# Spectral stage of a MetaFormer block: the mixed spectrum is turned in blocks on VectorE instead of passing through DRAM, and the mixing is interleaved with the next unit's x products

## The chip, the cores and the metric

One NeuronCore of one Trainium2 chip. The metric is the device time of one launch in microseconds; the kernel before is given by the median of three runs.

## What is computed

The input x is (32 images, 64 channels, 56x56), float32. The reference, cut to what matters:

```python
x = x + conv_ref(ln_c(x), ...)          # binary 3x3 convolution, batch norm, residual
t = tokens(x)                           # (32, 3136, 64)
t = t + ffn_ref(ln_t(t), ...)
# ffn_ref, for each of 4 branches i (the first T, T/2, T/4, T/8 tokens):
#   U_plus  = irfft(rfft(phi, 4096) * rfft(u, 4096))[:, :sl]        for 16 filters
#   U_minus = the same with u * (-1)^t, times (-1)^t afterwards
#   out_i   = sum_k s_k U_plus_k @ M_plus[i, k] + s_k U_minus_k @ M_minus[i, k]
#             + sum_{j<3} shift(u, j) @ M_u[i, j]
# and the output is a sum over branches with one-hot weights
```

The kernel does the length-4096 transforms in two steps, 128 rows (64 slots) by 32. In between, at each frequency, the spectrum of x (32 images by 64 channels) is multiplied by a 64x64 complex matrix that is itself put together from 35 filters.

## The kernel before, in words

The program has four parts, one after the other: `prepare` (constants, filters), `norm_and_convolve` (both norms, the convolution, the first transform step; it leaves the result in DRAM as z), `mix_frequencies` (the part that the change touches) and `finish` (the last transform step, the sum with the residual, the output).

`mix_frequencies` (L905 to L1247) first folds the four branches' matrices into m_sta (L1118 to L1128 on TensorE, L1204 on ScalarE, L1242 on VectorE). Then it goes through 32 units. A unit is two slots, 64 complex frequencies (NF = 64). Its work is cut into chunks of one PSUM bank (512 float32 columns), in the order that PLAN (L871) gives:

- p_v (L1058): the filters' spectrum for the unit; VectorE scales it in two instructions (L1150, L1153) to v_mov.
- x, 4 chunks (L1066): the second forward step of x, 4 matmuls of 128 columns each, array used as 128x128. Four copies a chunk (L1168) take the bank apart into xf.
- h, 16 chunks (L1071): the filter products, 8 float16 matmuls of 128 columns each, on two column tiles (L1078). One copy a chunk (L1172) into hf, 128x512.
- inv, 4 chunks, of the unit two before (LAG_INV = 2): the first inverse step, 16 matmuls of 512 columns on tiles of 32 rows and 64 columns (L1105). Copied to wf (L1178).
- mix, 4 chunks (L1082): at each frequency xf times hf, 16 matmuls of 128 columns a chunk on four tiles of 32 columns (L1090). Copied to y_sb (L1175).

In the trace each float32 matmul appears as two MATMUL instructions, so a mix chunk is 32 of them, an x chunk 8, the inverse step 32.

The seven banks of `ring` are used in turn: chunk p writes bank p % 7 and waits until the chunk seven before it has been copied (`bank_free`, L1033). Chunks with even p are copied by ScalarE, odd p by VectorE (`saver`, L1139). Each engine does its chunks in the order of the plan; TensorE issues its own strictly in that order too, so a matmul that waits holds back all that come behind it.

The mixed spectrum needs its frequencies on the partitions for the inverse step. Before, this goes through DRAM: y_sb is stored to y_scratch (L964), and read back in another order into yt (L969), two buffers of each. These are 1 MB out and 1 MB in for each unit, on SyncE's queue, which also loads the next z (L957), the constants fwd and inv (L958, L961) and, once, after the first two units, four tiles of the residual (L990, `load_x1`). GpSimd stores wf to w_scratch in 8 DMAs a unit (L1020), waits for their landing and then raises w_free (L1024), for which the next copy into the one wf waits (L1161).

For the last units the head of a unit (p_v, x, h, mix) is over before the tail (inv), so two steps with nothing but an inverse step come at the end.

Of the kernel before, what the change touches and what calls it, by code (L numbers as in the profile page):

```python
# [88 lines left out]
def constants():  # L89
# [44 lines left out]
    inv = inv.transpose(0, 1, 4, 2, 3, 5).reshape(NUNIT, 2 * NALPHA, 128)  # L134
    inv = np.concatenate([inv, inv], 1)
# [735 lines left out]
PLAN = [("x", 4), ("h", 16), ("inv", 4), ("mix", 4)]  # L871
TAIL = ("inv",)
LAG_INV = 2
RING = 7


def unit_chunks():

    seen, out = {}, []
    for stage, count in PLAN:  # L880
        for _ in range(count):
            k = seen.get(stage, 0)
            seen[stage] = k + 1
            out.append((stage, k, len(out)))
    return out


def chunk_is_there(stage, u):

    return (u >= LAG_INV) if stage in TAIL else (u < NUNIT)  # L890


def chunks_until(u, p, engine=None):


    plan = unit_chunks()
    if isinstance(u, int):
        return sum(1 for w in range(u + 1) for stage, _, at in plan
                   if chunk_is_there(stage, w) and (w < u or at <= p) and engine in (None, at % 2))
    per_unit = sum(1 for _, _, at in plan if engine in (None, at % 2))  # L900
    missing = LAG_INV * sum(1 for stage, _, at in plan if stage in TAIL and engine in (None, at % 2))
    return per_unit * u - missing + sum(1 for _, _, at in plan if at <= p and engine in (None, at % 2))


def mix_frequencies(nc, d, keep):  # L905


    chunks = unit_chunks()
    NCH = len(chunks)
    assert NCH % RING == 0 and NCH % 2 == 0  # L910
    pos = {(s, k): p for s, k, p in chunks}
    with ExitStack() as own:
# [8 lines left out]
        inv = [sb(f"inv{i}", [128, 2, 2 * NA]) for i in range(2)]  # L921
# [16 lines left out]
        y_stored = [sem(f"y_stored{i}") for i in range(2)]  # L938
        y_loaded = [sem(f"y_loaded{i}") for i in range(2)]
        chunk_ready, v_ready, v_saved, w_stored, w_free = (  # L940
            sem(n) for n in ("chunk_ready", "v_ready", "v_saved", "w_stored", "w_free"))
        sp_turn, pool_turn = sem("sp_turn"), sem("pool_turn")
# [12 lines left out]
        def _(sp):  # L955
# [4 lines left out]
            def load_inv(u, slot):  # L960
                sp.dma_start(inv[slot][:].rearrange("p r f -> p (r f)"), d["c_inv"][u]).then_inc(inv_loaded[slot], 16)  # L961

            def store_y(slot):
                sp.dma_start(d["y"][slot].rearrange("i p n -> p i n"), y_sb[slot][:]).then_inc(y_stored[slot], 16)  # L964

            def load_y(slot):
                for h in range(2):
                    src = d["y"][slot].rearrange("i (j m) n -> (i j) m n", j=4)[:, 16 * h:16 * h + 16, :]
                    sp.dma_start(yt[slot][64 * h:64 * h + 64].rearrange("p m r e -> p (m r e)"),  # L969
                                 src.rearrange("f m n -> f (m n)")).then_inc(y_loaded[slot], 16)  # L970
# [40 lines left out]
        def _(pool):  # L1011
            def store(u):

                for e in range(2):
                    pool.wait_ge(saved[e], chunks_until(u + LAG_INV, pos["inv", 3], e))
# [12 lines left out]
            with pool.Fori(1, NUNIT - LAG_INV) as u:  # L1028
                store(u)
            for u in range(NUNIT - LAG_INV, NUNIT):  # L1030
                store(u)

        def bank_free(eng, u, p):  # L1033

            if not isinstance(u, int):
                w, at = (u, p - RING) if p >= RING else (u - 1, p - RING + NCH)
                eng.wait_ge(saved[at % 2], chunks_until(w, at, at % 2))
                return
            before = [(w, at) for w in range(u + 1) for stage, _, at in chunks
                      if chunk_is_there(stage, w) and at % RING == p % RING and (w < u or at < p)]  # L1040
            if before:
                w, at = before[-1]
                eng.wait_ge(saved[at % 2], chunks_until(w, at, at % 2))
# [7 lines left out]
        def _(pe):  # L1051
            def unit(u, slot, use, head, tail):
# [7 lines left out]
                for stage, k, p in chunks:  # L1060
                    if not (tail if stage in TAIL else head):
                        continue
                    if stage != "inv":
                        bank_free(pe, u, p)
                    bank = ring[:, p % RING, :]
                    if stage == "x":  # L1066
                        for j in range(4):
                            at = CH * (8 * k + 2 * j)
                            mm = nc.tensor.matmul(bank[:, 128 * j:128 * j + 128], z_in[slot][:, at:at + 2 * CH],  # L1069
                                                  fwd[slot][:, NF:3 * NF], start=True, stop=True)  # L1070
                    elif stage == "h":  # L1071
# [3 lines left out]
                        for i in range(4):  # L1075
                            e = 4 * k + i
                            for n in range(2):
# [3 lines left out]
                                    tile_position=(0, CH * n))  # L1081
                    elif stage == "mix":  # L1082
                        if k == 0:
                            all_saved(pe, u, pos["h", 15])
                            if is_first(u):
                                pe.wait_ge(reals_done, 3)
                        for i in range(4):
                            for j in range(4):
                                f = 16 * k + 4 * i + j
                                mm = nc.tensor.matmul(bank[32 * j:32 * j + 32, 128 * i:128 * i + 128], xf[:, f, :],  # L1090
                                                      hf[:, f, :, :].rearrange("p r e -> p (r e)"),
                                                      start=True, stop=True, tile_position=(0, 32 * j))
                    else:
# [5 lines left out]
                        pe.wait_ge(y_loaded[slot], 32 * (use - 1))  # L1099
                        pe.wait_ge(inv_loaded[slot], 16 * (use - 1))  # L1100
                        for c in range(2):
                            for r in range(2):
                                for n in range(4):
                                    rows = slice(32 * n, 32 * n + 32)
                                    mm = nc.tensor.matmul(  # L1105
                                        ring[64 * c:64 * c + 64, pos["inv", n] % RING, :], inv[slot][rows, r, :],
                                        yt[slot][rows, 8 * c:8 * c + 8, r, :], start=(r == 0), stop=(r == 1),
                                        tile_position=(32 * n, 64 * c))
                                    if c and r:
# [364 lines left out]
```

## Time and profile before

| | us |
|---|---|
| median of 3 runs | 1436.41 |
| lowest, highest | 1433.49, 1443.66 |
| the profiled execution: time | 1433.59 |
| its span, first to last instruction | 1431.9 |
| mean granted TensorE clock in it | 0.931 of 2.4 GHz |

The profile was taken of one execution. Its busy figures are shares of the whole span, and mix the four parts, which have different limits; the unit loop lies at about 629 to 1182 us of the span. PE is TensorE's matmuls, DVE VectorE, ACT ScalarE, POOL GpSimd, SP SyncE. "idle before <- releaser" says how long an engine stood still ahead of an instruction and what ended that.

### The profile page before, as it was taken

To read this page: it belongs to the slowest core of one execution; us is meant where nothing else is said; L and a number is where in the kernel's file an instruction comes from. 1 tells how busy PE (TensorE), PEld (TensorE's weight loads), DVE (VectorE), ACT (ScalarE), POOL (GpSimd) and SP (SyncE) were. 2 spreads that over 40 slices of the span, in tenths; PEclk is the share of its full clock that TensorE was granted. 3 is DMA by queue.
4 is the path that set the end of the run, shared out by engine and by line. 5 is a ranking of instruction groups with operands and counts; after the bars stand their busy time and mean duration, and the time that the engine had idled before them with its cause. 6 is when DMAs were issued, how large, how long until landed. Compare 5 with 4: busy or idle time off the path is not lost. (4 is left out here: it accounts for less than half of the span.)

```text
span 1431.9 us, 37537 instructions
## 1 busy us (share of the span) xinstructions
PE 1174.5 (82%) x15089; PEld 779.4 (54%) x15089; DVE 954.0 (67%) x1420; ACT 798.9 (56%) x1487; POOL 498.9 (35%) x440
## 2 busy tenths in 40 slices
PE   1899999999999977688698998999899926865667
PEld 1455555555555543147577777777777713433334
DVE  5288888888888888636477777677777713433334
ACT  1787788778887853335366666566656612322223
POOL 2146556666655567200122332232232230000000
PEclk9999999999999988669899999999999977988778
DMA  7024545554455448426899999899989969978873
GB/s 228 1 91 133 166 155 182 188 162 149 154 181 172 149 133 185 140 82 187 263 281 300 270 283 299 272 275 291 291 267 284 284 177 359 406 313 341 327 314 135
DMA packets 179624, 317.66 MB, mean 222 GB/s; under 512 B 14805, under 2 KB 154423, under 8 KB 162935
## 3 DMA queue, kind: packets, MB, share of 16 engines
q1 hardware_dynamic: 164966, 257.47, 56.6%
q0 software_dynamic: 14592, 59.26, 11.8%
q8 instruction: 47, 0.77, 0.2%
q14 instruction: 19, 0.16, 0.0%
HBM read 162.93 MB, written 153.76 MB: 221 GB/s over the span
## 5 line engine op out<-in xcount | busy, mean ns | idle before, releaser
L1020 POOL DMA_DIRECT2D w_scratch<-wf x256 | 151.2, 594 | 430.5 <-ACT y_sb L1197 391.5
L491 POOL TENSOR_TENSOR u_t<-u_t,root 98x1024 f32<-98x1024 f32 x62 | 118.0, 1935 | 169.2 <-DVE root L799 169.2
L535 PE MATMUL ring_norm<-x_all,center 128*128 128x448 f32 (+2 forms) x384 | 148.1, 511 | 24.9 <-PEq L211 15.7
L1402 ACT ACTIVATE out_sb<-p_turn 128x392 f32<-128x392 f32 x128 | 62.7, 498 | 189.6 <-PE p_turn L1358 177.7
L1346 PE MATMUL p_out<-w_in,last_masked 128*98 128x512 f32 x256 | 141.2, 636 | 23.8 <-DMA w_in<-w_scratch 23.8
L1078 PE MATMUL ring<-v_mov,m_sta 105*64 105x128 f16 x4096 | 147.2, 221 | 14.3 <-DVE xf L1213 11.6
L1213 DVE COPY hf<-ring 128x512 f32<-128x512 f32 x256 | 156.1, 682 | 1.0
L1197 ACT ACTIVATE hf<-ring 128x512 f32<-128x512 f32 x256 | 144.7, 597 | 4.9
L1391 DVE TENSOR_TENSOR x_in<-p_out,x_in 98x512 f32<-98x512 f32 x96 | 65.4, 690 | 123.1 <-DMA x_in<-x_scratch 68.3
L594 PE MATMUL ring_norm<-u_t,step_masked 98*128 98x512 f32 x256 | 126.7, 623 | 21.9 <-POOL u_t L491 21.9
L1078 PEld LDWEIGHTS ring<-v_mov,m_sta 105*64 105x64 f16 x4096 | 119.9, 110 | 40.2 <-DVE xf L1213 16.8
L1090 PE MATMUL ring<-hf,xf 128*32 128x128 f32 x4096 | 123.3, 278 | 19.1 <-ACT wf L1197 8.8
L1090 PEld LDWEIGHTS ring<-hf,xf 128*32 128x32 f32 x4096 | 113.0, 112 | 45.0 <-issue 30.6
L491 POOL TENSOR_TENSOR xc_t<-xc_t,root 98x1024 f32<-98x1024 f32 x64 | 119.7, 1900 | 50.7 <-DVE root L799 50.7
L1197 ACT ACTIVATE xf<-ring 64x256 f32<-64x256 f32 x256 | 98.5, 385 | 66.8 <-PE ring L1069 64.5
L1213 DVE COPY xf<-ring 64x256 f32<-64x256 f32 x256 | 108.2, 423 | 32.4 <-PE ring L1069 28.1
L1069 PE MATMUL ring<-fwd,z_in 128*128 128x128 f32 x1024 | 122.2, 279 | 0.0
L1069 PEld LDWEIGHTS ring<-fwd,z_in 128*128 128x128 f32 x1024 | 121.7, 196 | 0.1
L535 PEld LDWEIGHTS ring_norm<-x_all,center 128*128 128x128 f32 x384 | 66.6, 192 | 84.5 <-issue 44.9
L1358 PEld LDWEIGHTS p_turn<-ident,x_in 98*128 98x128 f32 x384 | 47.1, 153 | 120.1 <-DVE x_in L1391 67.5
L567 PE MATMUL p_conv<-signs_padded,conv_w 64*64 64x392 bf16 x2304 | 109.2, 330 | 0.2 <-DVE x_all L755 0.2
L624 ACT ACTIVATE xc_t<-ring_norm 98x512 f32<-98x512 f32 x128 | 78.7, 615 | 46.1 <-PE ring_norm L546 46.1
(132 smaller groups left out, 1923.1 us busy)
## 6 DMA issues: line engine op xcount, KB each, us to landing
z_in<-z_scratch SPq DMA_DIRECT2D x32, 1076.5 KB, 9.7
z_scratch<-z_sb SPq DMA_DIRECT2D x16, 2048.0 KB, 8.9
y_scratch<-y_sb SPq DMA_DIRECT2D x32, 1024.0 KB, 12.7
yt<-y_scratch SPq DMA_DIRECT2D x64, 512.0 KB, 6.2
w_scratch<-wf POOLq DMA_DIRECT2D x256, 128.0 KB, 7.6
w_in<-w_scratch SPq DMA_DIRECT2D x8, 4096.0 KB, 15.8
x_all<-in_x SPq DMA_DIRECT2D x16, 1568.0 KB, 7.6
x_scratch<-x_t SPq DMA_DIRECT2D x16, 1568.0 KB
```

The lines of the kernel that those rows point to most:

```text
L491: return eng.tensor_tensor(v, v, r, ALU.mult)
L535: nc.tensor.matmul(bank_of("cen", q, c)[:, 0:WID * n], keep["center"][:, h, :], x_of(q)[:, WID * row:WID * row + WID * n], start=True, sto ...
L567: mm = nc.tensor.matmul(bank[CH * out:CH * out + CH, h, 0:CW], keep["conv_w"][CH * k:CH * k + CH, t, CH * k:CH * k + CH], pad[q % 2][CH * ...
L594: nc.tensor.matmul(bank_of("z", q, c), keep["step1"][:, c // 2, :], u_t[q % 2][:, c, :], start=True, stop=True).then_inc(z_ready, 1)
L624: nc.scalar.activation(xc_t[q % 2][:, c, :], bank, ACT.Copy).then_inc(xt_copied, 1)
L1020: nc.gpsimd.dma_start(w_units[u, h, s, c], wf[64 * c:64 * c + 64, 2 * h + s].rearrange("p (g n) -> p g n", n=256)).then_inc(w_stored, 16)
L1069: mm = nc.tensor.matmul(bank[:, 128 * j:128 * j + 128], z_in[slot][:, at:at + 2 * CH], fwd[slot][:, NF:3 * NF], start=True, stop=True)
L1078: mm = nc.tensor.matmul(bank[CH * n:CH * n + CH, 2 * NF * i:2 * NF * i + 2 * NF], m_sta[:, e, :], v_mov[:, NF * (1 - n):NF * (3 - n)], sta ...
L1090: mm = nc.tensor.matmul(bank[32 * j:32 * j + 32, 128 * i:128 * i + 128], xf[:, f, :], hf[:, f, :, :].rearrange("p r e -> p (r e)"), start= ...
L1197: return nc.scalar.activation(dst, src, ACT.Copy)
L1213: return nc.vector.tensor_copy(dst, src)
L1346: nc.tensor.matmul(p_out[0:NB, c % BANKS, :], keep["last"][:, ACH * c // MASKG, :], w_in[w_slot][:, ACH * c:ACH * c + ACH, 128 * slot:128 ...
```

## The change

The order of a step u becomes: p_v(u); then mix chunk k of unit u-1 and x chunk k of unit u in turn, for k = 0 to 3; then (on VectorE) four turns of the mixed spectrum of u-1; then the 16 h chunks of u; then the inverse step of u-1. The lag is one unit (LAG = 1), and one step with the tail alone is left at the end.

The four mix chunks stay in four PSUM banks (3 to 6), and VectorE turns them from there in 32x32 blocks into yt, a quarter of the channels in each of four `transpose` instructions of 512 elements in each partition. y_sb, y_scratch and their DMAs are gone. The inverse step is 8 matmuls of 512 columns on tiles of 64 rows and 64 columns, its constants are one tile of 64 columns. xf gets a second buffer, yt has one.

Banks and copying engines are given by tables; in `bank_free` a bank that held a mix chunk counts as free once the last turn is done. ScalarE copies x 0 and 2, eleven h chunks and inv 0 and 2; VectorE copies x 1 and 3, h 2, 5, 8, 11 and 14 and inv 1 and 3, and does the turns.

```diff
-PLAN = [("x", 4), ("h", 16), ("inv", 4), ("mix", 4)]
-TAIL = ("inv",)
-LAG_INV = 2
+TAIL = ("mix", "turn", "inv")
+LAG = 1
 RING = 7
+FIRST_MIX = 3
+H_ON_VECTOR = (2, 5, 8, 11, 14)
+BANKS = {"mix": (3, 4, 5, 6), "x": (0, 1, 2, 0), "h": (1, 2, 0, 1, 2, 0, 3, 4, 5, 6, 1, 2, 0, 3, 4, 5),
+         "inv": (6, 1, 2, 0)}
+def owner(stage, k):
+    if stage == "turn":
+        return 1
+    return int(k in H_ON_VECTOR) if stage == "h" else k % 2
+def step_chunks():
+    out = []
+    for k in range(4):
+        out += [("mix", k), ("x", k)]
+    out += [("turn", k) for k in range(4)]
+    out += [("h", k) for k in range(16)]
+    out += [("inv", k) for k in range(4)]
+    return [(stage, k, p) for p, (stage, k) in enumerate(out)]
...
-        xf = sb("xf", [128, NF, NIMG])
+        xf = [sb(f"xf{i}", [128, NF, NIMG]) for i in range(2)]
-        y_sb = [sb(f"y_sb{i}", [128, NF // 4, 2 * CH]) for i in range(2)]
-        yt = [sb(f"yt{i}", [128, NIMG // 2, 2, CH]) for i in range(2)]
+        yt = sb("yt", [128, CH, NIMG])
...
             def body(u, slot, use):
+                sp.wait_ge(chunk_ready, chunks_until(u, pos["x", 3]))
+                after_wait(sp, sp_turn)
                 if not known(u, NUNIT - 2, NUNIT - 1):
-                    sp.wait_ge(chunk_ready, chunks_until(u, pos["x", 3]))
-                    after_wait(sp, sp_turn)
                     load(u + 2, slot)
-                for e in range(2):
-                    sp.wait_ge(saved[e], chunks_until(u, pos["mix", 3], e))
-                after_wait(sp, sp_turn)
-                store_y(slot)
                 if not known(u, 0, 1):
                     load_inv(u, slot)
-                sp.wait_ge(y_stored[slot], 16 * use)
-                after_wait(sp, sp_turn)
-                load_y(slot)
...
+            stage, k, _ = chunks[at]
+            if stage == "mix":
+                stage, k, at = chunks[pos["turn", 3]]
+            eng.wait_ge(saved[owner(stage, k)], chunks_until(w, at, owner(stage, k)))
...
-                            all_saved(pe, u, pos["h", 15])
+                            all_saved(pe, u - 1, pos["h", 15])
-                                f = 16 * k + 4 * i + j
-                                mm = nc.tensor.matmul(bank[32 * j:32 * j + 32, 128 * i:128 * i + 128], xf[:, f, :],
+                                f = 16 * j + 4 * k + i
+                                mm = nc.tensor.matmul(bank[32 * j:32 * j + 32, 128 * i:128 * i + 128],
+                                                      xf[1 - slot][:, f, :],
+                                                      hf[:, f, :, :].rearrange("p r e -> p (r e)"),
...
-                        pe.wait_ge(y_loaded[slot], 32 * (use - 1))
-                        pe.wait_ge(inv_loaded[slot], 16 * (use - 1))
-                        for c in range(2):
-                            for r in range(2):
-                                for n in range(4):
-                                    rows = slice(32 * n, 32 * n + 32)
-                                    mm = nc.tensor.matmul(
-                                        ring[64 * c:64 * c + 64, pos["inv", n] % RING, :], inv[slot][rows, r, :],
-                                        yt[slot][rows, 8 * c:8 * c + 8, r, :], start=(r == 0), stop=(r == 1),
-                                        tile_position=(32 * n, 64 * c))
+                        pe.wait_ge(saved[1], chunks_until(u, pos["turn", 3], 1))
+                        pe.wait_ge(inv_loaded[1 - slot], 16 * (use if slot else use - 1))
+                        after_wait(pe, pe_turn)
+                        for h in range(2):
+                            for c, row in ((0, 0), (1, 1), (1, 0), (0, 1)):
+                                images = slice(16 * h + 8 * c, 16 * h + 8 * c + 8)
+                                rows = slice(64 * row, 64 * row + 64)
+                                mm = nc.tensor.matmul(
+                                    bank_of("inv", 2 * h + row)[64 * c:64 * c + 64, :],
+                                    inv[1 - slot][rows, :], yt[rows, :, images],
+                                    start=True, stop=True, tile_position=(64 * row, 64 * c))
...
-                    if p % 2 != which or not (tail if stage in TAIL else head):
+                    if (stage, k) not in mine or not (tail if stage in TAIL else head):
                         continue
-                    eng.wait_ge(chunk_ready, chunks_until(u, p))
+                    eng.wait_ge(chunk_ready, chunks_until(u, pos["mix", 3] if stage == "turn" else p))
                     if (stage, k) == ("inv", first_inv):
-                        eng.wait_ge(w_free, u - 1)
+                        eng.wait_ge(w_free, u)
...
-                        copy(y_sb[slot][:, 4 * k:4 * k + 4, :].rearrange("p i n -> p (i n)"), bank
+                    elif stage == "turn":
+                        e = slice(16 * k, 16 * k + 16)
+                        nc.vector.transpose(
+                            yt[:, e, :], ring[:, FIRST_MIX:FIRST_MIX + 4, :]
+                            .rearrange("p b (i r e) -> p e r (b i)", r=2, e=CH)[:, e]).then_inc(saved[which], 1)
+                    else:
+                        copy(wf[:, k, :].rearrange("p (i e) -> p i e", e=CH), bank.rearrange("p (e i) -> p i e", e=CH)
                              ).then_inc(saved[which], 1)
```

## Rows read from the trace of the kernel before

**Rows 1.** The page: busy time of TensorE; granted clock and DMA share in 40 slices

```profile
PE 1174.5 (82%) x15089; PEld 779.4 (54%) x15089; DVE 954.0 (67%) x1420; ACT 798.9 (56%) x1487; POOL 498.9 (35%) x440
...
PEclk9999999999999988669899999999999977988778
DMA  7024545554455448426899999899989969978873
```

**Rows 2.** Busy time of each engine, clock, DMA share, GB/s: 100 us of units

```profile
900.00:1000.00 100.00, 90.99 (x2021) 76.28 (x2021) 74.55 (x144) 62.99 (x131) 31.14 (x53) 1.00 0.91 281
```

**Rows 3.** Timeline of one unit: start us, us, engine line op, what, count [idle before]

```profile
868.37 0.57 PE L1058 MATMUL p_v<-fwd,z_in 128*105 128x192 f32 x2
...
868.78 3.73 PE L1069 MATMUL ring<-fwd,z_in 128*128 128x128 f32 x32
...
869.87 1.57 ACT L1197 ACTIVATE xf<-ring 64x256 f32<-64x256 f32 x4 [1.64 <-PE ring L1069]
...
870.76 3.52 DVE L1213 COPY xf<-ring 64x256 f32<-64x256 f32 x8 [0.79 <-PE ring L1069]
...
872.44 1.53 PE L1078 MATMUL ring<-v_mov,m_sta 105*64 105x128 f16 x48
873.26 4.65 ACT L1197 ACTIVATE hf<-ring 128x512 f32<-128x512 f32 x8
874.31 4.88 DVE L1213 COPY hf<-ring 128x512 f32<-128x512 f32 x8
...
878.42 2.01 PE L1105 MATMUL ring<-yt,inv 32*64 32x512 f32 x32 [0.93 <-DVE hf L1213]
...
880.36 3.70 PE L1090 MATMUL ring<-hf,xf 128*32 128x128 f32 x128
...
880.64 1.29 DVE L1213 COPY wf<-ring 128x512 f32<-128x512 f32 x2 [1.45 <-PE ring L1105]
...
883.99 0.57 PE L1058 MATMUL p_v<-fwd,z_in 128*105 128x192 f32 x2
```

**Rows 4.** Timeline, TensorE, same unit: last start of x, inverse step, mix

```profile
872.24 0.28 PE L1069 MATMUL ring<-fwd,z_in 128*128 128x128 f32 x1
...
879.75 0.67 PE L1105 MATMUL ring<-yt,inv 32*64 32x512 f32 x8
...
883.76 0.29 PE L1090 MATMUL ring<-hf,xf 128*32 128x128 f32 x4
```

**Rows 5.** The page, costliest groups: the convolution on tiles of 64x64

```profile
L567 PE MATMUL p_conv<-signs_padded,conv_w 64*64 64x392 bf16 x2304 | 109.2, 330 | 0.2 <-DVE x_all L755 0.2
```

**Rows 6.** Timeline, TensorE, the first five units

```profile
628.69 0.97 PE L1058 MATMUL p_v<-fwd,z_in 128*105 128x192 f32 x2 [1.56 <-DVE m_sta L1242]
...
643.06 3.70 PE L1090 MATMUL ring<-hf,xf 128*32 128x128 f32 x128 [2.51 <-DVE hf L1187]
646.69 0.57 PE L1058 MATMUL p_v<-fwd,z_in 128*105 128x192 f32 x2
...
682.49 2.36 PE L1090 MATMUL ring<-hf,xf 128*32 128x128 f32 x39 [4.85 <-issue]
...
709.57 1.94 PE L1090 MATMUL ring<-hf,xf 128*32 128x128 f32 x32 [8.27 <-ACT wf L1197]
...
728.14 0.57 PE L1058 MATMUL p_v<-fwd,z_in 128*105 128x192 f32 x2
```

**Rows 7.** Timeline, the end of the stage: last copies and store of wf, first load of `finish`

```profile
1170.69 1.29 DVE L1213 COPY wf<-ring 128x512 f32<-128x512 f32 x2 [8.58 <-PE ring L1105]
...
1172.56 4.68 POOL L1020 DMA_DIRECT2D w_scratch<-wf  x8 [5.17 <-DVE wf L1213]
1182.29 0.81 SPq L1284 DMA_DIRECT2D w_in<-w_scratch  x2
```

**Rows 8.** Clock after a wait: the timeline's matmuls, then engines and clock of 1 us

```profile
657.66 5.37 PE L1090 MATMUL ring<-hf,xf 128*32 128x128 f32 x128 [1.85 <-DVE hf L1213]
...
659.00:660.00 1.00, 1.00 (x25) 1.00 (x21) 0.00 (x0) 0.60 (x1) 0.00 (x0) 0.50 0.92 258
```

More of the change, by code:

```diff
@@ L888, in chunk_is_there @@
 def chunk_is_there(stage, u):
-    return (u >= LAG_INV) if stage in TAIL else (u < NUNIT)
+    return (u >= LAG) if stage in TAIL else (u < NUNIT)
 def chunks_until(u, p, engine=None):
-    plan = unit_chunks()
+    if engine is None:
+        mine = [(stage, at) for stage, k, at in step_chunks() if stage != "turn"]
+    else:
+        mine = [(stage, at) for stage, k, at in step_chunks() if stage != "mix" and owner(stage, k) == engine]
     if isinstance(u, int):
-        return sum(1 for w in range(u + 1) for stage, _, at in plan
-                   if chunk_is_there(stage, w) and (w < u or at <= p) and engine in (None, at % 2))
@@ L900, in chunks_until @@
-    per_unit = sum(1 for _, _, at in plan if engine in (None, at % 2))
-    missing = LAG_INV * sum(1 for stage, _, at in plan if stage in TAIL and engine in (None, at % 2))
-    return per_unit * u - missing + sum(1 for _, _, at in plan if at <= p and engine in (None, at % 2))
+        return sum(1 for w in range(u + 1) for stage, at in mine
+                   if chunk_is_there(stage, w) and (w < u or at <= p))
+    missing = LAG * sum(1 for stage, at in mine if stage in TAIL)
+    return len(mine) * u - missing + sum(1 for stage, at in mine if at <= p)
@@ L905, in mix_frequencies @@
 def mix_frequencies(nc, d, keep):
-    chunks = unit_chunks()
-    NCH = len(chunks)
-    assert NCH % RING == 0 and NCH % 2 == 0
+    chunks = step_chunks()
     pos = {(s, k): p for s, k, p in chunks}
@@ L1027, in _, with bank_of @@
             store(0)
-            with pool.Fori(1, NUNIT - LAG_INV) as u:
+            with pool.Fori(1, NUNIT - LAG) as u:
                 store(u)
-            for u in range(NUNIT - LAG_INV, NUNIT):
+            for u in range(NUNIT - LAG, NUNIT):
                 store(u)
+        def bank_of(stage, k):
+            return ring[:, BANKS[stage][k], :]
         def bank_free(eng, u, p):
+            stage, k, _ = chunks[p]
+            same = [at for other, n, at in chunks if other != "turn" and BANKS[other][n] == BANKS[stage][k]]
             if not isinstance(u, int):
[L1036 to L1041, printed above, removed]
+                w, at = (u, max(at for at in same if at < p)) if min(same) < p else (u - 1, max(same))
+            else:
+                before = [(w, at) for w in range(u + 1) for at in same
+                          if chunk_is_there(chunks[at][0], w) and (w < u or at < p)]
+                if not before:
+                    return
                 w, at = before[-1]
-                eng.wait_ge(saved[at % 2], chunks_until(w, at, at % 2))
+            stage, k, _ = chunks[at]
+            if stage == "mix":
+                stage, k, at = chunks[pos["turn", 3]]
+            eng.wait_ge(saved[owner(stage, k)], chunks_until(w, at, owner(stage, k)))
         def all_saved(eng, u, p):
@@ L1060, in unit @@
                 for stage, k, p in chunks:
-                    if not (tail if stage in TAIL else head):
+                    if stage == "turn" or not (tail if stage in TAIL else head):
                         continue
@@ L1064, in unit @@
                         bank_free(pe, u, p)
-                    bank = ring[:, p % RING, :]
+                    bank = bank_of(stage, k) if stage != "inv" else None
                     if stage == "x":
@@ L1130, in _ @@
             two_by_two(pe, NUNIT, body)
[L1131 to L1132 removed]
+            unit(NUNIT, NUNIT % 2, NUNIT // 2 + 1, False, True)
         def m_part(c):
@@ L1139, in saver @@
         def saver(eng, which, copy):
-            mine = [(stage, k) for stage, k, p in chunks if p % 2 == which]
+            mine = [(stage, k) for stage, k, p in chunks if stage != "mix" and owner(stage, k) == which]
             first_inv = min(k for stage, k in mine if stage == "inv")
-            first_mix = min(k for stage, k in mine if stage == "mix")
             last_h = max(k for stage, k in mine if stage == "h")
@@ L1205, in _ @@
             unit = saver(act, 0, copy)
-            two_by_two(act, NUNIT, lambda u, slot, use: unit(u, slot, use, True, not known(u, 0, 1)))
-            for u in (NUNIT, NUNIT + 1):
-                unit(u, u % 2, u // 2 + 1, False, True)
+            two_by_two(act, NUNIT, lambda u, slot, use: unit(u, slot, use, True, not known(u, 0)))
+            unit(NUNIT, NUNIT % 2, NUNIT // 2 + 1, False, True)
         @block.vector
@@ L1244, in _ @@
             unit = saver(dve, 1, copy)
-            two_by_two(dve, NUNIT, lambda u, slot, use: unit(u, slot, use, True, not known(u, 0, 1)))
-            for u in (NUNIT, NUNIT + 1):
-                unit(u, u % 2, u // 2 + 1, False, True)
+            two_by_two(dve, NUNIT, lambda u, slot, use: unit(u, slot, use, True, not known(u, 0)))
+            unit(NUNIT, NUNIT % 2, NUNIT // 2 + 1, False, True)
 def finish(nc, d, keep):
```

57 lines of the change are left out of this document (17 added, 40 removed).

## The prediction

> **What bounds the kernel now.** I read the page's slices first: the clock and the DMA share [rows 1] show a stage with the clock at full and the DMA engines nine tenths busy, the unit loop. Then the engines over 100 us of it [rows 2]: TensorE 91%, VectorE 75%, ScalarE 63%, DMA share 0.91. The DMA is loaded but ends nothing in the steady part; what does, the timeline of one unit says [rows 3]. From one p_v to the next it is 883.99 - 868.37 = 15.62 us, all of it TensorE's chain: p_v 0.41, x 3.66, h with its waits 5.98 (872.44 to 878.42), inverse step 1.94, mix 3.63. The waits inside are short, 0.93 us at most. So in the steady part the trip of y through DRAM costs nothing: it lies beside a chain of matmuls.
>
> It costs at the ends. In the first five units [rows 6] there are idle times of 4.85 and 8.27 us; from 646.69 to 728.14 there are four units, 81.45 us where four times 15.62 is 62.5: 19.0 us are lost, while the residual's four tiles and y share the DMA engines. At the end two steps with a tail alone wait for y. The whole stage, first p_v to the first load of `finish`, is 1182.29 - 628.69 = 553.6 us [rows 6, 7].
>
> **The change, a step at a time.** Time 0 is the start of p_v, warm clock.
>
> TensorE's slots. The 32 x instructions start from 868.78 to 872.24 [rows 3, 4], a pitch of 0.1116, so a chunk of 8 is 0.89. Mix: 124 instructions from 880.36 to 883.76, 0.0274 each, 0.88 a chunk of 32 (0.89 taken). h is 48 in 1.53 less the last one's length, 0.028 each: 0.225 a chunk of 8. The inverse step keeps its number of rounds: 8 tiles of 32x64 with 32 instructions, now 4 tiles of 64x64 with 16; four rounds of 0.43 either way, 1.75. That four 64x64 tiles do run at once the convolution bears out: 109.2 us / 2304 = 47 ns for 392 columns [rows 5].
>
> Change of tile shape. Over and above the pitch, the first matmul of the next kind comes late by 872.44 - 872.24 - 0.11 = 0.09 (x to h), 883.99 - 883.76 - 0.11 = 0.12 (mix to p_v), 880.36 - 879.75 - 0.43 = 0.18 (inverse to mix) [rows 3, 4]. I take 0.10. There are four such changes in a unit now, eleven in the new step. The Trainium skill (TensorEngine Tiling (Array Packing), Key Properties) says that changing the tiling mode drains TensorE; this speaks against alternating mix and x, and by the rows the seven added drains are 0.7 us a step, at 0.18 each 1.3. The trace agrees that there is a price, and puts it at these tenths.
>
> First part, to the end of the last x chunk: 0.1 + 0.37 + 4 x 0.89 + 4 x 0.89 + 8 x 0.10 = 8.4 us. The two waits in it are covered: banks 0 to 2 are free of the inverse chunks by then, x 3 needs x 0's bank, copied at 4.2.
>
> Then comes what I think decides. VectorE has its work in this order: v_mov, x 1, x 3, the four turns, and only then h 2. The pieces in line:
> - x 3 is ready at 8.6 (0.2 after its last slot, as 869.87 is after the first chunk's [rows 3]); four copies at 3.52 / 8 = 0.44 each: 10.3.
> - Four turns, 512 elements each from PSUM. No row shows one. The nearest is VectorE's copy of 512 elements out of PSUM, eight in 4.88, 0.61 each [rows 3]; I take 0.62, to 12.8. Below, the 256-element copy at 0.44 (18.4 a step instead of 19.2); above, a turn that reads its block first and writes it after, twice the copy, 1.22 (21.6 a step). The Trainium skill (Vector Engine (DVE) Microarchitecture Reference, section 3.8) has the block transpose sustain one element per cycle per lane; as an estimate from that page a turn is some 0.53 us and the step 18.8. No run here shows it yet.
> - h 2's copy: 13.4. TensorE meanwhile issued h 0 and h 1 (to 8.9), stood until x 3's bank 0 came free (10.4), issued h 2 to h 4 (to 11.1), and stands again: h 5 needs bank 0, which h 2 holds, whose copy is behind the turns. It starts at 13.5. Everything behind h 5 waits with it, also h 6 to h 9, whose banks 3 to 6 the turns freed.
> - From there ScalarE sets the pace: h 6, 7, 9, 10 and 12 at 0.58 each (4.65 us for eight [rows 3]) from 13.9: h 12 is copied at 17.0. The inverse step needs the banks of h 9 to h 12, starts 0.4 later (now 0.4 lie between h 11's copy and it: 874.31 + 5 x 0.60 + 0.68 = 878.0 against 878.42 [rows 3]), and takes 1.75 to 19.2.
>
> So a step is 19.2 us against 15.62. VectorE is busy only some 12 us of it and ScalarE 11; it is their order, not their load, that makes 5.3 us of TensorE's idle time in a step.
>
> The edits that come out at nothing: y's store and load, hidden now, so nothing gained in a steady unit; load_inv and the next z are issued after x 3 with a whole step to land; the copies into wf have the same shape as before (0.60 a copy, strided reads are there in h's already); v_mov is done at 1.7 and needed at 8.5. SyncE loses a wait, which frees nobody. GpSimd's eight stores are ready a step before w_free is wanted.
>
> **Sum over the stage.** Step 0 has no tail: from p_v to the first mix after it 643.06 - 628.69 = 14.4 us before [rows 6], the same now within a few tenths (14.2: the next p_v goes ahead of that wait). 31 steps of P follow. Then the step with a tail alone: mix 3.9, turns 2.5, inverse step 2.3. Its copy into wf waits for the store before it (ready 1.8 after the step starts, 4.7 to issue [rows 7], some 5 to land: 11.8), copies end at 13.1, and from last copy to `finish` it is 10.3 (1182.29 less 1170.69 + 1.29 [rows 7]): 23.4. The stage is 37.6 + 31 P. The 19.0 us lost at the start aren't in it: with y's 2 MB a unit gone, I take the residual's tiles to find room. With P = 19.2 it is 632.8, 79 more than 553.6. It would break even at P = 16.6.
>
> The clock. It is at 2.4 GHz through the units, with a wait of 0.9 in each. After a wait of 1.85 us it went to 1.2 GHz once, and the mix took 5.37 instead of 3.70, 1.67 more [rows 8]; after one of 2.51 it stayed up [rows 6]. The new step has waits of 1.5 and 2.4 us with only 0.7 us of matmuls between them, and 1.4 more ahead of the inverse step. Bounds: nothing, or 1.67 in each step. The slow stretch would fall first on the h products, where ScalarE sets the pace and half speed costs little, so I take 0.7. P = 19.9, the stage 37.6 + 616.9 = 654.5, 100.9 more.
>
> The profiled execution took 1433.6 (2.8 below the median, 0.2%): 1433.6 + 100.9 = 1534.5, and I say 1535 us.
>
> **Rivals.**
> A. The same chain, clock at 2.4 GHz throughout: P = 19.2, 1433.6 + 79 = 1513 us. For it: the 2.51 us wait after which the clock held. Against: here two waits come together, in every step.
> B. The clock falls and stays low into the inverse step and the next mix: P = 20.9, the stage 685.5, 1565 us. For: the 1.67 measured.
> C. A turn costs twice a copy: P = 21.6 + 0.3 of clock, the stage 716, 1596 us. For: nothing in the trace but that the operation is new; the copies' rate is the likelier guide.
> D. Faster. The turns are hidden, h isn't held, and TensorE runs on as now; 15.62 + 0.7 for shape changes = 16.3, the stage 543, 1423 us. The gain is then the DMA's at both ends. It needs 2.6 us off the chain from x 3's copy to h 12's copy, so turns and copies on VectorE that overlap far more than the 0.61 pitch shows. Against: VectorE's order is written down, and h 5's bank hangs on it.
> E. It doesn't do what it says, DMA load stays: the DMA's waits return at the start, 19 us on the forecast, 1554. Inside the range and hardly likely, as the stores are deleted.
>
> **Numbers.** Forecast 0.39, A 0.22, B 0.18, C 0.09, D 0.07, E 0.02; 0.03 for about no change, which lies between D and A. The range from 1488 (turns at 0.44 and a held clock: P = 18.4) to 1590 leaves out D, most of C and no change. A difference of 1% (14 us) is about what can be told from none: slower 0.90, same 0.03, faster 0.07.
>
> **What would show it.** Right: p_v to p_v near 20 us; TensorE waiting for VectorE's hf copy ahead of an h product for over 2 us in each step, and for its xf copy for 1.5; transposes near 0.68 each, four in 2.5; ScalarE's h copies in two bunches; DMA share about half; clock under 1.0 in a part of each step; no idle time of 4 us or more in the first units. Wrong: h products that run without those waits, transposes of 1.2, or a step under 17 us.

## The result, and the profile after

The changed kernel takes 1557.68 us, median of 4 runs (1557.04 to 1558.24), against 1434.95 for the one before in the same rounds: a ratio of 1.0843, 95% interval 1.0802 to 1.0885. It is slower, by 8%, where 1535 was forecast (range 1488 to 1590).

The page of the changed kernel, the lines that answer to [rows 1]:

```profile
PE 1253.8 (81%) x14577; PEld 824.8 (53%) x14577; DVE 944.0 (61%) x1388; ACT 812.8 (52%) x1519; POOL 499.2 (32%) x440
...
PEclk9999999999999875788888888888888886988878
DMA  7025546464555473263333334333333326988883
```

and 200 us of steps, to set beside [rows 2] (busy us of TensorE, its weight loads, VectorE, ScalarE, GpSimd; clock; DMA share; GB/s):

```profile
800.00:1000.00 200.00, 164.86 (x2964) 130.32 (x2956) 111.89 (x206) 100.20 (x205) 43.41 (x74) 0.85 0.36 109
```

The DMA share fell from 0.91 to 0.36: the change does what it says. VectorE has less to do per microsecond than before (56% against 75%), ScalarE too, and TensorE is idle or slow. The clock, 1.00 in the units before, is 0.85.

The timeline of one step says where the time went (start us, length us, engine, line, operation, count, idle before and its releaser); it answers to [rows 3]:

```profile
894.56 0.57 PE L1060 MATMUL p_v<-fwd,z_in 128*105 128x192 f32 x2
...
900.27 1.16 PE L1071 MATMUL ring<-fwd,z_in 128*128 128x128 f32 x8
...
901.36 1.08 PE L1094 MATMUL ring<-hf,xf 128*32 128x128 f32 x32
...
902.37 1.16 PE L1071 MATMUL ring<-fwd,z_in 128*128 128x128 f32 x8
...
903.46 0.64 PE L1081 MATMUL ring<-v_mov,m_sta 105*64 105x128 f16 x16
...
903.57 1.73 DVE L1215 COPY xf<-ring 64x256 f32<-64x256 f32 x4 [2.47 <-PE ring L1071]
...
905.33 2.51 DVE L1176 STREAM_TRANSPOSE yt<-ring 128x512 f32<-128x512 f32 x4
...
905.35 0.86 PE L1081 MATMUL ring<-v_mov,m_sta 105*64 105x128 f16 x24 [1.25 <-DVE xf L1215]
...
907.76 0.65 DVE L1215 COPY hf<-ring 128x512 f32<-128x512 f32 x1
...
908.47 4.90 PE L1081 MATMUL ring<-v_mov,m_sta 105*64 105x128 f16 x88 [2.26 <-DVE hf L1215]
...
913.30 2.15 PE L1111 MATMUL ring<-yt,inv 64*64 64x512 f32 x16
...
915.38 0.57 PE L1060 MATMUL p_v<-fwd,z_in 128*105 128x192 f32 x2
```

VectorE copies x 3 (1.73), turns (2.51), copies h 2 (0.65), in one row without a gap; TensorE waits first for the x 3 copy (1.25 us) and then for h 2's (2.26), and only at 908.47 goes on with h 5. Those are the two waits of the forecast. Steps come in a cycle of 19.96, 20.82 and 20.65; nine of them from 1078.87 to 1263.19 make 20.48 each, against 15.62 before.

The clock of single microseconds of that step: around the second wait, among the h products and in the next p_v:

```profile
906.00:907.00 1.00, 0.21 (x8) 0.05 (x2) 1.00 (x3) 0.97 (x2) 0.00 (x0) 0.96 1.00 422
907.00:908.00 1.00, 0.00 (x0) 0.00 (x0) 1.00 (x3) 0.11 (x1) 0.00 (x0) 0.50 0.96 398
...
912.00:913.00 1.00, 1.00 (x24) 1.00 (x22) 0.41 (x2) 0.87 (x2) 0.00 (x0) 0.50 0.00 0
915.00:916.00 1.00, 1.00 (x14) 0.38 (x10) 0.83 (x2) 0.74 (x2) 0.00 (x0) 1.00 0.00 0
```

It falls to 1.2 GHz just before 907, within the second wait, stays there past 913, through h 5 to h 15, and is back at 2.4 for the float32 products. The h products at half clock take 4.90 us for 11 chunks, 0.44 a chunk; so TensorE, not the copies, sets the pace there. The waits are the same in every step, and the low stretch is not: about 6.3 us here, 6.8 in the step of 20.65, and 3.9 in the one of 19.96, where the clock falls at about 889.9, behind the wait and in the middle of the h products:

```profile
888.51 3.71 PE L1081 MATMUL ring<-v_mov,m_sta 105*64 105x128 f16 x88 [2.26 <-DVE hf L1215]
...
892.15 2.48 PE L1111 MATMUL ring<-yt,inv 64*64 64x512 f32 x16
```

The ends of the stage, which answer to [rows 6, 7]: the first p_v, a wait for GpSimd's store of wf, the first load of `finish`.

```profile
628.37 0.97 PE L1060 MATMUL p_v<-fwd,z_in 128*105 128x192 f32 x2 [1.56 <-DVE m_sta L1244]
...
689.22 2.08 PE L1071 MATMUL ring<-fwd,z_in 128*128 128x128 f32 x8 [3.04 <-DVE wf L1215]
...
1303.99 0.80 SPq L1285 DMA_DIRECT2D w_in<-w_scratch  x2
```

The stage takes 1303.99 - 628.37 = 675.6 us, 122.0 more than before; the whole execution 1557.15, 123.6 more than the one before. All of the loss is in this stage.

### The profile page after: what moved, and what is told of

It reads as the page before. It is cut to its first block and busy times, and to the rows that moved or that the text cites. A ratio compares the mean times of both kernels' runs of the same rounds, so it can differ in the third digit from the quotient of the medians.

```text
span 1554.8 us, 36484 instructions
## 1 busy us (share of the span) xinstructions
PE 1253.8 (81%) x14577; PEld 824.8 (53%) x14577; DVE 944.0 (61%) x1388; ACT 812.8 (52%) x1519; POOL 499.2 (32%) x440
## 5 line engine op out<-in xcount | busy, mean ns | idle before, releaser
L1081 PE MATMUL ring<-v_mov,m_sta 105*64 105x128 f16 x4096 | 189.6, 271 | 110.3 <-DVE hf L1215 70.3
L1200 ACT ACTIVATE hf<-ring 128x512 f32<-128x512 f32 x352 | 190.1, 598 | 144.0 <-PE ring L1081 143.4
L1081 PEld LDWEIGHTS ring<-v_mov,m_sta 105*64 105x64 f16 x4096 | 171.6, 145 | 124.7 <-DVE hf L1215 75.5
L1071 PE MATMUL ring<-fwd,z_in 128*128 128x128 f32 x1024 | 152.4, 294 | 3.0 <-DVE wf L1215 3.0
L1215 DVE COPY hf<-ring 128x512 f32<-128x512 f32 x160 | 109.2, 684 | 65.9 <-PE ring L1081 65.7
L1071 PEld LDWEIGHTS ring<-fwd,z_in 128*128 128x128 f32 x1024 | 128.6, 197 | 27.9 <-issue 24.4
L1094 PE MATMUL ring<-hf,xf 128*32 128x128 f32 x4096 | 139.3, 278 | 1.8 <-DVE hf L1190 1.8
L1094 PEld LDWEIGHTS ring<-hf,xf 128*32 128x32 f32 x4096 | 105.4, 110 | 21.9 <-issue 8.0
```

What stands on the lines that cost most here:

```text
L1081: mm = nc.tensor.matmul(bank[CH * n:CH * n + CH, 2 * NF * i:2 * NF * i + 2 * NF], m_sta[:, e, :], v_mov[:, NF * (1 - n):NF * (3 - n)], sta ...
L1200: return nc.scalar.activation(dst, src, ACT.Copy)
L1215: return nc.vector.tensor_copy(dst, src)
```

## The experiments

Theory: the order of VectorE's queue (x 3, four turns, h 2) holds up h 5 and all behind it, and the waits let the clock fall. Rivals: the alternation of tile shapes, the amount of work on VectorE, the DMA.

**e1_h_owner: no h copy behind the turns**

```diff
-H_ON_VECTOR = (2, 5, 8, 11, 14)
+H_ON_VECTOR = (7, 9, 11, 13, 15)
```

> The changed kernel with one table altered: VectorE copies h chunks 7, 9, 11, 13 and 15 instead of 2, 5, 8, 11 and 14, so that no h chunk that comes before h 6 has its copy behind the four turns. If VectorE's queue order is the cause, the wait of 2.3 us ahead of h 5 goes, one of under 1 us is left ahead of h 6 (banks 3 to 6 come free with the last turn), and a step falls from 20.5 to about 18.4 us: 1557.7 - 31 x 2.1 = 1493 us. If the alternation of tile shapes or the mere amount of work on the copying engines is the cause (the amounts are the same), the time stays within 10 us of 1557.7.

Measured: 1544 us (1537 and 1551), ratio 1.0743 (1.0657 to 1.0829) to the kernel before. 14 us gained where 65 were expected, and the two runs lie 14 apart. The timeline has the reason. The waits did change as expected, 1.26 ahead of h 2, 0.24 ahead of h 5, 1.02 ahead of h 6 for the last turn. But the steps come in two kinds. From 706.10 to 874.96 they are 18.2 and 19.2 in turn, nine of them 18.76 on average; from 895 on they grow from 20.29 to 20.48 and stay there. Clock and busy times of a stretch of either kind, and of one step of 18.2:

```profile
820.00:857.00 37.00, 31.37 (x604) 24.59 (x608) 22.19 (x42) 20.36 (x42) 9.42 (x16) 0.95 0.41 123
...
762.75:780.97 18.22, 15.11 (x311) 11.67 (x307) 11.10 (x21) 9.97 (x21) 4.72 (x8) 1.00 0.41 125
...
1017.00:1058.00 41.00, 35.96 (x620) 27.52 (x612) 22.99 (x43) 20.84 (x43) 9.43 (x16) 0.83 0.37 111
```

The h products from h 6 on, in a step of 19.2, in one of 18.2 and in one of 20.29:

```profile
756.89 4.05 PE L1081 MATMUL ring<-v_mov,m_sta 105*64 105x128 f16 x80 [1.02 <-DVE yt L1176]
...
776.08 2.42 PE L1081 MATMUL ring<-v_mov,m_sta 105*64 105x128 f16 x80 [1.02 <-DVE yt L1176]
...
908.39 4.48 PE L1081 MATMUL ring<-v_mov,m_sta 105*64 105x128 f16 x80 [1.02 <-DVE yt L1176]
...
912.79 2.61 PE L1111 MATMUL ring<-yt,inv 64*64 64x512 f32 x16
```

The same program, with the same waits: in the steps of 18.2 the clock does not fall at all, in those of 19.2 it is low for some 3.4 us, in the later ones for some 6.8 us, all the h products from h 6 on and a part of the inverse step (2.61 against 1.95). The 18.4 that was expected is met by the steps at full clock. At 20.48 the later steps are no shorter than the changed kernel's: there the low clock costs 20.48 - 18.22 = 2.26 us and takes back the whole gain. What the order is worth can't be read from this run beside the changed kernel's, since both order and clock differ; e2_filled and e7_owner_filled hold the clock.

**e2_filled: the clock held**

```diff
+WARM = {2: 5, 5: 9}
...
+                    if stage == "h" and k in WARM:
+                        for _ in range(WARM[k]):
+                            nc.tensor.matmul(p_v[:, 256:384], keep["center"][:, 0, :], keep["center"][:, 0, :],
+                                             start=True, stop=True)
```

> The changed kernel with matmuls that nobody reads put into TensorE's two waits, five 128-column float32 ones ahead of h 2 and nine ahead of h 5, 1.1 and 2.0 us where it stood for 1.25 and 2.26. If the low clock on the h products is a cost of those waits, the granted clock stays at 1.00 through the step, h 5 to h 15 go at ScalarE's pace again, and a step falls by 0.9 to 1.3 us: 1557.7 - 31 x 1.1 = about 1524 us. If the clock costs nothing because the copies set the pace anyway, the time stays within 8 us of 1557.7.

Measured: 1523.9 us, ratio 1.0602 (1.0537 to 1.0667); 1524 was expected. Each step is 19.27 (999.82 to 1192.51 are ten). The end of one step, the h products after the filled wait in the next, and the clock:

```profile
898.78 3.54 ACT L1205 ACTIVATE hf<-ring 128x512 f32<-128x512 f32 x7 [2.03 <-PE ring L1086]
...
901.61 1.95 PE L1116 MATMUL ring<-yt,inv 64*64 64x512 f32 x16 [0.86 <-ACT hf L1205]
...
917.40 2.65 PE L1086 MATMUL ring<-v_mov,m_sta 105*64 105x128 f16 x88
```

```profile
917.00:920.00 3.00, 2.95 (x92) 2.64 (x90) 2.49 (x5) 1.92 (x4) 0.00 (x0) 1.00 0.14 40
```

88 instructions take 2.65 us, not 4.90, and now the copies set the pace: the inverse step waits 0.86 us for ScalarE. h 2 and h 5 start as far behind p_v as without the unneeded matmuls (10.79 and 13.91), so these held up nothing. Work that nobody needs made the kernel 34 us faster. So of the 4.86 us that a step has lost, 1.21 are the clock, and 3.65 are there at full clock.

**e7_owner_filled: both**

The edit is e1_h_owner's table in e2_filled, with `WARM = {2: 5, 6: 4}`.

> e1_h_owner and e2_filled together: no h copy behind the turns ahead of h 7, and five and four matmuls that nobody reads ahead of h 2 and of h 6, to hold the clock. e1_h_owner alone shortened TensorE's waits by 1 us a step and gained nearly nothing, its steps 20.48 us with the h products at the low clock. If that was the clock, here it is 1.00 and the step some 17.6 us against e2_filled's 19.27: 1523.9 - 31 x 1.65 = 1473 us. If the order of the copies was never worth anything, it stays at 1524 within 10.

Measured: 1492.1 us, ratio 1.0395 (1.0373 to 1.0418). A step is 18.24 (1002.23 to 1148.12 are eight), 1.03 below e2_filled's; 1.65 was expected. The direction is right and the size is not. With the clock held the copies' order is worth a microsecond a step, and 31 x 1.03 = 32 us is what was measured. The steps of e1_h_owner in which the clock did not fall, 18.22, say the same. It does not clear the path, since h 6 still waits for the turns, which hold banks 3 to 6:

```profile
905.09 1.16 PE L1068 MATMUL p_v<-center 128*128 128x128 f32 x8
...
906.18 2.42 PE L1086 MATMUL ring<-v_mov,m_sta 105*64 105x128 f16 x80
```

**e3_turns_twice: the turns doubled**

```diff
-                        nc.vector.transpose(
-                            yt[:, e, :], ring[:, FIRST_MIX:FIRST_MIX + 4, :]
-                            .rearrange("p b (i r e) -> p e r (b i)", r=2, e=CH)[:, e]).then_inc(saved[which], 1)
+                        for dst in (spare, yt):
+                            ins = nc.vector.transpose(
+                                dst[:, e, :], ring[:, FIRST_MIX:FIRST_MIX + 4, :]
+                                .rearrange("p b (i r e) -> p e r (b i)", r=2, e=CH)[:, e])
+                        ins.then_inc(saved[which], 1)
```

> The changed kernel with each of the four turns made twice, the first time into a tile that nobody reads: 2.5 us more on VectorE in each step. If the turns lie in the one chain that sets the step, the step grows by 1.7 to 2.5 us and the time by 53 to 80 us, to 1611 to 1638. If they lie beside something longer, the time stays within 15 us of 1557.7.

Measured: 1646.8 us, ratio 1.1458 (1.1385 to 1.153), 89 above the changed kernel, 9 over the upper end. The clock's mean fell from 0.887 to 0.866 in it. TensorE's wait ahead of h 5 is 4.65 us instead of 2.26, so the 2.5 us of four turns are on the path nearly in full, and the clock, lower in the mean, goes with the rest: 89 / 32 = 2.8 us a step.

**e5_not_alternating: shapes in blocks, clock held**

```diff
-    for k in range(4):
-        out += [("mix", k), ("x", k)]
+    out += [("mix", k) for k in range(4)]
+    out += [("x", k) for k in range(4)]
     out += [("turn", k) for k in range(4)]
```

This on top of e2_filled.

> e2_filled (clock held by matmuls that nobody reads) with the four mix chunks first and the four x chunks after them; the turns stay behind x 3 on VectorE, all tables as they are. This takes six of the changes of tile shape out of a step and moves nothing else in the chain. From e2_filled's trace p_v to h 0 is 8.90 us; with blocks as e4_turn_under_x has them (0.50 + 3.63 + 3.92) it is 8.05. Expected: a step of 18.4 us where e2_filled has 19.27, and 1523.9 - 31 x 0.85 = 1497 us. If the shape changes are hidden behind the copies, 1524 within 6.

Measured: 1506.7 us (1500 and 1513), ratio 1.0496 (1.0438 to 1.0554). A step is 18.75 (1006.25 to 1137.50 are seven), 0.52 under e2_filled's; 0.85 was expected. One step of the trace shows where the rest went:

```profile
893.75 0.57 PE L1061 MATMUL p_v<-fwd,z_in 128*105 128x192 f32 x2
...
903.66 2.51 DVE L1181 STREAM_TRANSPOSE yt<-ring 128x512 f32<-128x512 f32 x4
...
904.95 2.27 PE L1068 MATMUL p_v<-center 128*128 128x128 f32 x18
906.10 0.65 DVE L1220 COPY hf<-ring 128x512 f32<-128x512 f32 x1
...
907.15 2.65 PE L1086 MATMUL ring<-v_mov,m_sta 105*64 105x128 f16 x88
```

The turns start 9.91 us after p_v, where the changed kernel has 10.77: 0.86 earlier, as expected, 0.14 for each of the six changes. But h 5 starts only 0.51 earlier. The copy that frees its bank ends at 906.75, and the nine unneeded matmuls, written for the longer wait, run on to 907.2. So the step understates what the changes of shape cost. The two runs lie 13 us apart, and nothing on record says why; the step is read from the faster one. The changes of shape count, and they are the smaller part of the 3.65 us.

**e6_y_sixteenth: the kernel before, nearly without y**

```diff
-                store_y(slot)
+                part = 16 if known(u, 0, 1) else 1
+                store_y(slot, part)
...
-                load_y(slot)
+                load_y(slot, part)
```

From the third unit on the inverse step reads old values in most of yt.

> The kernel before, with y stored and loaded in full for the first two units only and a sixteenth of it from the third on, so the inverse step of later units reads old values in most of yt: 1.9 MB less DMA in each unit. If y's trip is hidden in the steady part, as the prediction has it, a unit stays at 15.6 us and only the start (19.0 us lost) and the end gain, together 10 to 30 us: 1437 goes to 1407 to 1427. If the DMA load slows the units themselves, a unit falls below 15.4 and the time below 1400.

Measured: 1429.9 us, ratio 0.994 (0.9916 to 0.9963). A unit is 15.59 (1011.61 to 1136.30 are eight), as before. The trip through DRAM costs nothing in the steady part; that half of the expectation held. The other did not, and 1430 lies above the 1407 to 1427 that was expected: the start is as bad as it was, although y is gone from the third unit on:

```profile
682.48 1.85 PE L1092 MATMUL ring<-hf,xf 128*32 128x128 f32 x39 [4.03 <-issue]
...
711.94 1.94 PE L1092 MATMUL ring<-hf,xf 128*32 128x128 f32 x32 [9.69 <-ACT wf L1199]
```

**e4_turn_under_x: the turns beside the x products**

```diff
-    for k in range(4):
-        out += [("mix", k), ("x", k)]
+    out += [("mix", k) for k in range(4)]
     out += [("turn", k) for k in range(4)]
+    out += [("x", k) for k in range(4)]
...
-H_ON_VECTOR = (2, 5, 8, 11, 14)
+H_ON_VECTOR = (3, 5, 7, 9, 11)
...
-"x": (0, 1, 2, 0), "h": (1, 2, 0, 1, 2, 0, 3, 4, 5, 6, 1, 2, 0, 3, 4, 5),
-         "inv": (6, 1, 2, 0)}
+"x": (2, 0, 1, 2), "h": (3, 4, 5, 6, 0, 1, 2, 3, 4, 5, 6, 0, 1, 2, 3, 4),
+         "inv": (5, 6, 0, 1)}
```

> All four mix chunks first, then the four x chunks: VectorE turns the mixed spectrum while TensorE makes x, and TensorE finds banks 3 to 6 free when h begins. h chunks go through the seven banks in turn, VectorE copies h 3, 5, 7, 9 and 11. If the place of the turns in VectorE's queue is the cause, TensorE's waits of over 1 us are gone, the clock stays at 1.00, and a step is about 15.5 us: 1557.7 - 31 x 5.0 = 1403 us, faster than both kernels. If only the changes of tile shape count, six fewer at under 0.2 us each, it is 1557.7 - 31 x 1.1 = 1524 us.

Measured: 1414.2 us, ratio 0.9839 (0.9787 to 0.9891): 9% under the changed kernel and 1.6% under the one before. The step is 15.59, the clock 1.00 in it. The turns run while TensorE makes x:

```profile
907.78 3.98 PE L1071 MATMUL ring<-fwd,z_in 128*128 128x128 f32 x32
907.92 2.51 DVE L1176 STREAM_TRANSPOSE yt<-ring 128x512 f32<-128x512 f32 x4 [2.65 <-PE ring L1094]
...
913.86 2.56 PE L1081 MATMUL ring<-v_mov,m_sta 105*64 105x128 f16 x80 [0.64 <-DVE xf L1215]
...
917.36 1.95 PE L1111 MATMUL ring<-yt,inv 64*64 64x512 f32 x16 [0.94 <-DVE hf L1215]
```

The same instructions do the same work; only their places and the tables differ. It is 11 us over the expected 1403. The step gained 4.89 us and not 5.0, 3.4 us over 31 steps, and the start loses 13.9 us where the changed kernel lost 8.5. Most of that start is one wait, 10.11 us ahead of a mix chunk in step 3 (for a copy into wf, which waited for GpSimd's store while the residual's tiles were loading).

**e8_x1_spread and e9_before_x1_spread: the residual's loads spread**

```diff
             for n in range(len(PREFETCHED)):
+                for u in (2 + 2 * n, 3 + 2 * n):
+                    body(u, u % 2, u // 2 + 1)
                 load_x1(n)
-            with sp.Fori(1, NUNIT // 2 - 1) as h:
+            with sp.Fori(5, NUNIT // 2 - 1) as h:
```

on e4_turn_under_x, and the same on the kernel before.

> e4_turn_under_x with the four loads of the residual's tiles spread, one behind the units 3, 5, 7 and 9 on SyncE's queue instead of all four behind unit 1. In e4_turn_under_x TensorE stood once for 10.1 us ahead of a mix chunk, because the copies into wf waited for GpSimd's store while those loads were under way. Expected: no wait of over 2 us in the first ten units, the time 8 to 12 us lower, 1414 to 1404 us. If the stall was not from those loads, 1414 within 4.

> The kernel before with the four loads of the residual's tiles spread as in e8_x1_spread, y's trip through DRAM as it was. If those loads alone make the stalls of the first units, the 19 us lost there go and the time falls by 10 to 19 us, to about 1420; the step stays 15.6. Then 1420 less 1400 is what e8_x1_spread owes to the turns on VectorE: the end of the stage. If y's share of the DMA engines (0.91 in the units) is the reason, spreading helps little, and the time stays within 6 of 1436.

Measured: e8_x1_spread 1400.1 us, ratio 0.9745 (0.9722 to 0.9768), 14 less, and from 657 to 740 us of its trace, where the long wait had been, TensorE stands for 1.00 us at most. e9_before_x1_spread 1440.3, ratio 1.0029 (1.0001 to 1.0056): no gain, against my theory of the loads alone. The long wait became several, two of those on SyncE's own transfers:

```profile
763.53 1.93 PE L1092 MATMUL ring<-hf,xf 128*32 128x128 f32 x32 [3.17 <-ACT wf L1199]
...
776.36 2.01 PE L1107 MATMUL ring<-yt,inv 32*64 32x512 f32 x32 [1.26 <-DMA yt<-y_scratch]
...
800.91 0.96 PE L1060 MATMUL p_v<-fwd,z_in 128*105 128x192 f32 x2 [0.95 <-DMA fwd<-in_c_fwd]
```

Put together, what the 30 steps behind the second p_v lost beyond 30 steady ones: 20 us in the kernel before, 21 with y nearly gone, 23 with the loads spread, 14 in e4_turn_under_x (no y, the new order, the loads in one lump), 2 in e8_x1_spread (both, and the new order). So at the start it takes both; e9_before_x1_spread and e6_y_sixteenth alone won nothing there. The four loads are 1568 KB each, and at the 281 GB/s of [rows 2] that is, as an estimate, some 22 us of transfers, which is about what was lost. That the DMA engines, nine tenths busy, had no room for them wherever they were put, and that without y the lump stalls the stores, fits this and was not tested apart.

This is half of the 36 us between 1436 and 1400. The other half, 17 us, lies in the first step and behind the last p_v: 18.0 + 48.2 = 66.2 us before, 11.2 + 37.8 = 49.0 in e8_x1_spread. The kernel before has two tails there, and they stand 1.71 and 13.12 us for y from DRAM:

```profile
1166.84 3.69 PE L1105 MATMUL ring<-yt,inv 32*64 32x512 f32 x32 [13.12 <-DMA yt<-y_scratch]
```

**e10_inverse_in_halves: the inverse step waits in two pairs**

```diff
-                        for at in range(4):
-                            bank_free(pe, u, pos["inv", at])
...
-                        after_wait(pe, pe_turn)
                         for h in range(2):
+                            for at in (2 * h, 2 * h + 1):
+                                bank_free(pe, u, pos["inv", at])
+                            after_wait(pe, pe_turn)
```

on e8_x1_spread.

> e8_x1_spread with the inverse step waiting for its four banks in two pairs, the first pair ahead of the first four matmuls and the second ahead of the others, instead of for all four at once. TensorE stands for 0.94 us there in each step. If the last pair's copies are what it waits for, 0.3 to 0.5 us of it goes: 1400 - 31 x 0.4 = 1388 us. If the first pair is late already, or the next wait (the last h copy ahead of the mixing) takes it back, 1400 within 4.

Measured: 1375.6 us, ratio 0.9589 (0.9552 to 0.9627). The step is 14.79 (1012.21 to 1086.17 are five), 0.80 less, twice what was expected: of the 0.94 ahead of the inverse step 0.14 is left, and nothing behind it takes the gain back.

```profile
906.80 1.95 PE L1113 MATMUL ring<-yt,inv 64*64 64x512 f32 x16
```

## Why the prediction was right, and where it was off

The mechanism held at each point but one, what the low clock costs. From p_v, in the step of 894.56 and in the forecast:

| | forecast | measured |
|---|---|---|
| h 0 issued | 8.5 | 8.90 |
| x 3's copies end, turns start | 10.3 | 10.77 |
| four turns | 2.5 | 2.51 |
| h 5 issued | 13.5 | 13.91 |
| inverse step starts | 17.4 + 0.7 for the clock | 18.74 (17.39 in e2_filled) |
| next p_v | 19.9 | 20.82 (20.48 on average) |

- The price of a turn was taken from VectorE's copy of the same size out of PSUM, 0.62; it is 2.51 / 4 = 0.63. Rival C (a turn at twice a copy) is out. So is the estimate of 0.53 made from the Trainium skill (Vector Engine (DVE) Microarchitecture Reference, section 3.8): in this case the turn has the copy's pitch, and the measurement decides.
- The change of tile shape was taken at 0.10. In the timeline x to mix is 901.36 - 900.27 = 1.09 for a chunk of 0.89, 0.20 over, and mix to x 902.37 - 901.36 = 1.01 against 0.88, 0.13 over. That is the 0.4 in the first row. e5_not_alternating puts the six changes at 0.86, 0.14 each. The Trainium skill (TensorEngine Tiling (Array Packing), Key Properties) has a change of mode drain the engine; the trace agrees that each change costs time, these tenths, and does not show a drain as such.
- The clock was the term mis-sized: 0.7 a step taken, within bounds of nothing and 1.67. e2_filled shows 1.21. The wrong step was "the slow stretch would fall first on the h products, where ScalarE sets the pace and half speed costs little": at half clock a chunk takes TensorE 0.44, and the copies' joint pace is 0.32 (ScalarE's seven in 3.54 us for eleven chunks, in e2_filled); in the steps of 20.82 and 20.65 the low clock covers them all. With the clock held the sum is right: 19.27 against rival A's 19.2, with the wait for ScalarE's last copy where the forecast had it, 0.86 for 1.4. Rival B's 1.67 is a little nearer to 1.21 than 0.7 is, but its mechanism was not seen: the clock stays low into the inverse step in some steps, and never into the next mix in the steps read.
- The start: the forecast took the 19.0 us lost there as won back. Steps 1 and 3 took 23.61 and 25.83, so 8.5 of them are still lost, and in e8_x1_spread, with the tiles' loads spread, 2 are.
- The ends gave 5 us more than forecast: step 0 took 12.4 instead of 14.2, and from the last step to `finish` 20.0 instead of 23.4. There the copies into wf had to wait for the store before them until 8.5 us into the tail, not 11.8.
- Together: 31 steps are 643.3 (20.75 each with the stalls) instead of 616.9, the ends 32.4 instead of 37.6; 675.6 against 654.5. That two terms erred in opposite directions brought the total 5 us nearer by luck.
- Two small slips in the sums change nothing: 19.2 less four times 0.18 is 18.5, not 18.4 (the lower end 1490, not 1488), and 1.8 + 4.7 + 5 is 11.5, not 11.8.
- Rival D needed the turns hidden from the chain. e4_turn_under_x is that kernel, by another order, and its 1414 stands beside the 1423 that the rival was given. That is in part luck: its step is 15.59 and not 16.3, and it loses 14 us at the start that the rival did not count.
- That the trip through DRAM is hidden in a steady unit was right (e6_y_sixteenth: 15.59). That its gain lies at both ends was right too; at the start it was had only with the residual's loads spread as well.

What stays open: why the clock in e1_h_owner fell in every other step for nine steps, for 3.4 us, and in every step for 6.8 us later, and why the changed kernel has a cycle of three. The runs show the patterns and what each costs, not what picks one.

## What to carry to other kernels

An engine's queue is a path: before work is moved to an engine with time to spare, write down what it does just before and just after, and who waits for the last item. Here 2.5 us of turns stood between two copies that TensorE waited for; with the clock that fell in these waits and the added changes of shape that cost 8%. The same turns beside the x products made the kernel 1.6% faster than the one before, with the residual's loads spread 2.5%, and with one wait split in two 4%. Where an engine's waits let its clock fall, judge a change of order with the clock held, or its gain can vanish into the clock; and taking a hidden transfer away may win little by itself: it was 6 us here, and the 18 lost at the start came back only with the new order and the other loads moved as well.

## What the runs showed of the hardware that I had not expected

- VectorE's 32x32 block transpose of 128x512 float32 out of PSUM, read with a stride of 128 columns and across four banks, goes at 0.63 us a piece in a row, the same as a plain copy of that size (0.61).
- With waits of 1.25 and 2.26 us and 0.86 us of matmuls between them, TensorE's clock fell to 1.2 GHz in every step read, in one within the second wait and in another 1.4 us behind it, and stayed there for 3.9 to 6.8 us. Fourteen unneeded float32 matmuls of 128 columns in the waits held it at 2.4 GHz and took 34 us off the kernel.
- The same program, with the same waits, ran steps of 18.22 us (clock never low) and 19.20 (low for 3.4 us) in turn for a while, and of 20.48 (low for 6.8 us) for the rest of the stage.
- One wait for four banks, split in two pairs, gave 0.80 us a step where 0.94 had been idle: 24 us of 1400.
